# A graph network layer pair: one-hots of the first stage on VectorE in three wide instructions per tile, those of the second in two per two pairs, and a ring reported by quarters

## The reference

```python
def layer0(h, src, dst):                      # GIN
    agg = segment_sum(h[src], dst)            # rows gathered by src, summed by dst
    z = (1.0 + eps_gin) * h + agg
    z = relu(z @ W1 + b1) @ W2 + b2
    z = (z - z.mean(0)) * rsqrt(z.var(0) + 1e-5) * gamma + beta
    return z + h

def layer1(x, row, col, val):                 # here row = src, col = dst
    support = segment_sum(val[:, None] * x[col], row)
    return relu(support @ weight)

x = layernorm(x + layer0(x, src, dst))
x = layernorm(x + layer1(x, src, dst, edge_weight))
```

## Time and profile before

| | |
|---|---|
| timed runs | 4326.99, 4327.98, 4332.28 us; median 4327.98 us |
| span of the profiled execution | 5351.1 us, 79415 instructions; no time other than its span is given for it |
| busy in the profile | PE 3721.5, POOL 3177.6, DVE 2301.2, ACT 1495.5 us |
| granted PE clock, mean | 0.83 of 2.4 GHz |
| gathers | 1664 in stage 1, 1612 in stage 2 |
| moved by DMA | 541 MB, 101 GB/s on the mean |

### The profile page before, as it was taken

The page is one execution under the profiler, slowest core; times in us unless marked ns, Lnnn a source line. Parts: engine busy times, 40 slices in busy tenths (PEclk is TensorE's granted clock), DMA queues, the critical chain, the costliest instruction groups (busy, mean ns, idle before and its releaser), DMA issues.

```text
span 5351.1 us, 79415 instructions
## 1 busy us (share of the span) xinstructions
PE 3721.5 (70%) x16131; PEld 3045.6 (57%) x16132; DVE 2301.2 (43%) x5448; ACT 1495.5 (28%) x4377; POOL 3177.6 (59%) x3352
## 2 busy tenths in 40 slices
PE   2677676667667776767742667777777777777777
PEld 2565555555555655656632556566665666665666
DVE  2545454545555544545563233333333333333333
ACT  2444444445444444444552000000000000000001
POOL 6666655565656665666335666666666666666662
PEclk6887888888887878888855789888888888888898
DMA  4333333333333333333293333333333333333331
GB/s 134 93 97 92 99 90 97 90 97 93 95 93 97 93 97 91 96 97 99 62 298 123 90 94 99 96 101 96 100 101 99 95 100 100 102 97 97 100 100 53
DMA packets 298112, 541.14 MB, mean 101 GB/s; under 512 B 77802, under 2 KB 190302, under 8 KB 297838
## 3 DMA queue, kind: packets, MB, share of 16 engines
q0 software_dynamic: 159424, 434.52, 28.3%
q10 hardware_dynamic: 89348, 67.77, 4.0%
q1 hardware_dynamic: 49066, 36.39, 2.2%
HBM read 489.80 MB, written 46.88 MB: 100 GB/s over the span
## 4 chain that ended last, share of the span: by engine, by line
issue 27%; ACTq 16%; another core or an unknown queue 15%; PE 15%; ACT 12%; DVE 9%; DVEq 4%; DMA 2%; SPq 1%; POOL 0%; PEldq 0%; POOLq 0%
PE ps L1419 10%; ACT ones_sb L1613 7%; DVE work L1096 7%; ACTq L1611 4%; ACTq L1613 2%; DVEq L1096 2%; PE ps L1221 2%; ACT ring L1611 2%; ACTq L1642 1%; PE ps L1459 1%; ACT ones_sb L1619 1%; ACTq L1617 1%; ACTq L377 1%; PE ps L1292 1%
## 5 line engine op out<-in xcount | busy, mean ns | idle before, releaser
L548 POOL DMA_INDIRECT ring<-in_x,idx x1664 | 1587.9, 954 | 1039.5 <-issue 456.4
L606 POOL DMA_INDIRECT ring<-x_dram,idx x1612 | 1528.0, 948 | 904.9 <-issue 479.8
L1419 PE MATMUL ps<-ring,work 128*128 x6448 | 1631.3, 411 | 581.1 <-DVE work L1096 387.5
L1419 PEld LDWEIGHTS ps<-ring,work 128*128 128x128 f32 x6448 | 1327.7, 208 | 851.0 <-issue 649.4
L1221 PE MATMUL ps<-ring,ones_sb 128*128 x3708 | 1115.7, 449 | 454.8 <-ACT ones_sb L1619 301.9
L1096 DVE TENSOR_SCALAR work<-ps,dstT,wT 128x256 f32<-128x256 f32 x1612 | 748.0, 536 | 1551.6 <-remote 977.0
L1221 PEld LDWEIGHTS ps<-ring,ones_sb 128*128 128x128 f32 x3708 | 800.4, 225 | 676.6 <-issue 550.2
L1613 ACT ACTIVATE ones_sb<-tile_nodes,dstT 128x128 f32<-128x128 f32 x1854 | 651.0, 391 | 396.5 <-issue 331.1
L1292 PE MATMUL ps<-work 128*128 128x128 f32 x3384 | 499.2, 301 | 203.6 <-issue 148.1
L1292 PEld LDWEIGHTS ps<-work 128*128 128x128 f32 x3384 | 484.0, 216 | 233.5 <-issue 189.8
L1791 ACT ACTIVATE work<-ps 128x512 f32<-128x512 f32 x49 | 29.3, 597 | 1764.2 <-remote 1111.7
(11 more groups left out here) (240 smaller groups left out, 2299.3 us busy)
## 6 DMA issues: line engine op xcount, KB each, us to landing
ring<-in_x,idx POOLq DMA_INDIRECT x1664
ring<-x_dram,idx POOLq DMA_INDIRECT x1612
z_dram<-z_pair ACTq DMA_DIRECT2D x49, 256.0 KB
ones_sb<-x_dram ACTq DMA_DIRECT2D x49, 256.0 KB
ring<-z_dram SPq DMA_DIRECT2D x24, 512.0 KB, 4.1
ring<-in_x SPq DMA_DIRECT2D x24, 512.0 KB, 5.6
x_dram<-ring ACTq DMA_DIRECT2D x24, 512.0 KB
out<-ones_sb ACTq DMA_DIRECT2D x48, 256.0 KB
```

Source lines behind the costliest of these rows:

```text
L548: nc.gpsimd.indirect_dma_start(out=ring[:, q, c, :], out_offset=None, in_=x, in_offset=bass.IndirectOffsetOnAxis(ap=idx[:, q, c:c + 1], ax ...
L606: nc.gpsimd.indirect_dma_start(out=ring[:, q, c, :], out_offset=None, in_=x1_dram, in_offset=bass.IndirectOffsetOnAxis(ap=idx[:, q, c:c + ...
L1419: last = nc.tensor.matmul(to[:, t * D:(t + 1) * D], ones_of[:, b, c, t * P:(t + 1) * P], ring[:, ds((p + b) & (RING - 1), 1), c, :].rearra ...
```

## The change

- Stage 1's one-hots move from ACT to DVE (`ones_of_tile` in the vector block). A one-hot is now `(dstT + tile_base) == minus_iota`, one instruction for many chunks, with the destinations and the node numbers broadcast: one instruction for the shared pair (256 elements per partition), one for all eight head pairs (2048), one for the last (256), and 512 elements per two loop pairs. The tile's `tile_base` is the scalar. They are made whether the tile has such pairs or not; the table's counts become fixed numbers per tile (`TILE_ONES` = 10).
- DVE makes the first half of `keyed(k - 1)`, then the one-hots of tile 2k+1, the second half, and after `take(k)` those of tile 2k+2. It waits for the sum of the tile two before.
- The self weights are copied by POOL, eight pairs at a time, from `self_next`, which SP loads beside `idx`.
- Stage 2: for two pairs one instruction `equal` over 1024 elements (bucket_nodes in PSUM, dstT in SBUF) and one product with wT in place, with a wait between; a wait for the heads of the bucket before stands ahead of the first four loop pairs.
- Four semaphores per ring instead of sixteen: SP reports eight pairs at a time. POOL waits for slots every four pairs.
- PE waits once for a tile's head one-hots and twice for its landed pairs (`low`, `end`). ACT's order becomes simpler.
- `table` and `table2` are 16-bit.

```diff
+        tile_base = sb("tile_base", [P, NT], f32)
+        minus_iota = sb("minus_iota", [P, P], f32)
+        self_next = sb("self_next", [P, RING, 2], f32)
...
-                        for g in range(RING // TWO):
-                            sp.wait_ge(s_gathered[g], r * (32 * TWO) + 32 * TWO)
-                            sp.sem_inc(s_landed, TWO)
...
+                        for g in range(4):
+                            sp.wait_ge(s_gathered[g], r * (32 * QUARTER) + 32 * QUARTER)
+                            stand(sp)
+                            sp.wait_ge(s_selfed, r * 4 + g + 1)
+                            sp.sem_inc(s_landed, QUARTER)
+                            if g % 2 == 1:
...
+                                sp.dma_start(self_next[:, h * HALF:(h + 1) * HALF, :],
+                                             selfT[:, ds((i + 1) * RING + h * HALF, HALF), :]).then_inc(s_idx[h], 16)
...
+            def selves_of(q, of):
+                nc.gpsimd.tensor_copy(ring_self[:, q:q + QUARTER, :], of[:, q:q + QUARTER, :]).then_inc(s_selfed, 1)
...
-                        if q % TWO == 0:
-                            pool.wait_ge(s_entered, r * RING + (q - RING + 3))
+                        if q % FOUR == 0:
+                            pool.wait_ge(s_entered, r * RING + (q - RING + FOUR + 1))
...
+                        if (q + 1) % QUARTER == 0:
+                            selves_of(q + 1 - QUARTER, self_next)
...
+            def ones_of_tile(j, bank):
+                new, head, m4, m2, _, _, _, shared, off, sweep = entry(dve, j)
...
+                def equal(to, at, n):
+                    return nc.vector.scalar_tensor_tensor(
+                        out=to.rearrange("p b c n -> p (b c) n"),
+                        in0=dstT[:, ds(at, n), :].rearrange("p b c -> p (b c)").unsqueeze(2).to_broadcast([P, 2 * n, P]),
+                        scalar=base, in1=minus_iota[:, :].unsqueeze(1).to_broadcast([P, 2 * n, P]), op0=ALU.add, op1=ALU.is_equal)
+                if not (isinstance(j, int) and j < 2):
+                    dve.wait_ge(s_acc, j - 1)
+                equal(shared_of[bank], shared, 1).then_inc(s_onehot, 1)
...
+                equal(heads_of[bank], head, BATCH)
+                equal(last_of[bank], m2, 1).then_inc(s_onehot, TILE_ONES - 1)
...
                 def weighted(to, p, n):
-                    for b in range(n):
-                        for c in range(2):
-                            last = nc.vector.tensor_scalar(to[:, b, c, :], bucket_nodes, dstT[:, ds(at + b, 1), c], wT[:, ds(at + b, 1), c],
-                                                           ALU.is_equal, ALU.mult)
-                    last.then_inc(s_onehot2, n)
+                    wide = [P, 2 * n, BUCKET]
+                    each = lambda of: of[:, ds(at, n), :].rearrange("p b c -> p (b c)").unsqueeze(2).to_broadcast(wide)
+                    nc.vector.tensor_tensor(flat_of, bucket_nodes.unsqueeze(1).to_broadcast(wide), each(dstT), ALU.is_equal).then_inc(s_equal2, n)
+                    dve.wait_ge(s_equal2, p + n)
+                    nc.vector.tensor_tensor(flat_of, flat_of, each(wT), ALU.mult).then_inc(s_onehot2, n)
...
+                pe.wait_ge(s_onehot, head + counted + TILE_ONES)
+                pe.wait_ge(s_landed, low + first)
```

More of the change, by code:

```diff
@@ L15 @@
 TWO = 2
+QUARTER = RING // 4
+FOUR = 4
 GROUP = 4
@@ L859, in take, with keyed @@
                 stand(dve)
-            def keyed(k):
-                for q in range(PARTS):
+            def keyed(k, parts):
+                for q in parts:
                     mine = slice(q * WIDTH, (q + 1) * WIDTH)
@@ L973, in block @@
                 if old >= 1:
-                    keyed(k - 1)
+                    keyed(k - 1, range(PARTS // 2))
+                ones_of_tile(2 * k + 1, 1)
+                if old >= 1:
+                    keyed(k - 1, range(PARTS // 2, PARTS))
                 if old >= 5:
@@ L987, in _ @@
                 block(k, 5, False)
-            keyed(NS - 1)
+            keyed(NS - 1, range(PARTS // 2))
+            ones_of_tile(2 * NS + 1, 1)
+            keyed(NS - 1, range(PARTS // 2, PARTS))
+            ones_of_tile(2 * NS + 2, 0)
+            ones_of_tile(2 * NS + 3, 1)
             regions_and_targets()
@@ L1206, in sum_tile @@
             def sum_tile(j, bank, others):
-                new, head, m4, m2, end, off, _, rep, _, _ = entry(pe, j)
+                new, head, m4, m2, end, low, rep, _, off, sweep = entry(pe, j)
+                first = sweep * RING
+                counted = first + off
                 if not (isinstance(j, int) and j < 2):
```

287 lines of the change are left out of this document (128 added, 159 removed).

## The result

The changed kernel takes **4579.17 us** (median of 4 runs, 4572.48 to 4589.37) against 4327.48 us before (4 runs): ratio **1.058** [1.057, 1.060], 252 us slower. The forecast was 358 us slower. The profiled execution's span is 4575.0 us, so this time the profile is a picture of the timed runs.

A forecast was written before the change was run, and what follows sets the result against it. POOL's gather issue (4108 us) was taken as the bound of the timed 4328 us; 342 for held gathers + 46 copies + 20 late reports - 50 spared waits = 358 us more, say 4685 us, range 4330 to 4830.

The forecast's parts named there:

- The 2048- and 256-element one-hots of stage 1: VectorE in stage 1: instructions with both inputs in SBUF hold POOL's gathers, 150 us plus 7 us on the mean.
- The product of stage 2: VectorE in stage 2: products with wT, both inputs in SBUF, hold POOL's gathers, 182 us plus 3 us for single pairs.
- The copies: POOL: 104 self-weight copies between gathers, each 0.14 us plus one gap of 0.30 us, 46 us; ends 15 and 130.
- The late quarters: Ring reports of eight pairs: PE sees the last six pairs of each stage later, 20 us (0 to 20).
- Recovered waits: POOL's waits for PE: a PE fed sooner spares some of 0 to 213 us, taken as 50 us less.
- What VectorE does more: VectorE's added work, to 1708 us in stage 1 and some 1060 in stage 2, is covered by POOL's gathers.
- The equal of stage 2: VectorE in stage 2: bucket_nodes in PSUM against dstT, so it holds no gather and is harmless.
- The wait between equal and product: VectorE in stage 2: 415 waits of at most 1.26 us, 523 us as upper end, still covered.
- (a): Rival: ScalarE's one-hots bound the timed runs, not gather issue; the change would be faster, 4243 us, chance 0.15.
- (b): Rival: gathers don't wait for the new two-SBUF instructions; 4344 us, chance 0.08.
- (c): Rival: gathers wait, but half of it hides in POOL's other waits; 4495 us, chance 0.13.
- (d): Rival: VectorE becomes the bound of stage 1 through dependent steps with waits, 98 us more, 4783 us, chance 0.10.

The follow-up runs named there:

- b2: Kernel before with only the ring changed: reports of eight pairs, slot waits every four pairs, both stages, 16-bit tables; 4358.97 us against 4338.23, ratio 1.0047.
- e2: Changed kernel with stage 1's one-hots reading the node numbers from PSUM instead of SBUF, same instructions and sizes; 4474.24 us, ratio 1.033 to before.
- e1: Changed kernel with stage 2's one-hots made as before, one instruction per chunk with bucket_nodes in PSUM; 4500.76 us, ratio 1.0395 to before.
- e5: Changed kernel with a 512-element PSUM-to-PSUM copy between stage 2's equal and product; 4737.03 us, ratio 1.0914 to before.
- b1: Kernel before with one operand of keyed's long compare (L870) moved from PSUM to SBUF, and 16-bit tables; 4404.99 us against 4330.5, ratio 1.0174.
- e3: Changed kernel with stage 2's old one-hots and stage 1's node numbers read from PSUM, both edits together; 4395.53 us, ratio 1.0146 to before.
- e6: Changed kernel with each self-weight copy cut into two halves without a wait, in the slow batch (before 5431.63 us); 5415.76 us, ratio 0.998.
- e9: Changed kernel with stage 1's 2048-element heads instruction cut into four of 512; 4519.7 us, ratio 1.0444 to before.
- e4: Changed kernel with each of POOL's 104 self-weight copies made twice, with a wait between; 4727.07 us, ratio 1.0896 to before.

## Why the prediction was right, and where it was not

The mechanism was the forecast one: POOL's gather issue is the bound, and gathers wait for VectorE's instructions with two operands in SBUF. Its sizes were not all right.

**The sum, term by term** (forecast, then measured):

- The 2048- and 256-element one-hots of stage 1: 157, measured 138 less the 12 of the kernel before (b2's gathers: 956 against 949 ns) = **126 us**. The phase average is near; e2 takes it away (the 128 us by which stage 1's last gather starts earlier).
- The product of stage 2: 185, measured **78 us** (e1 takes off 78). This is the term that was mis-sized. "Nothing ties one phase to the other for long, so I take the mean" is the step that failed: a held gather sets the phase anew, and at 2.48 us a couple the 245 products that follow another couple directly hold nothing; e5 makes the same products hold 231.
- The copies: 46, measured at most **19 us**: POOL's stage 1 has 25.4 us of copies (3 of them held ones) and 6.8 less idle time than b2's (504.3, 511.1), and of that 19 some 4 are more waiting for PE (13.4, 9.1). The step that took a copy for 0.14 us and a whole issue gap counted a gap that isn't there: the copy lies largely in the one that is.
- The late quarters: 20, measured **21 us** (b2), 13 of it the end and 5 the four further gathers; the size was right in part by luck, since the further gathers weren't in it.
- Recovered waits: -50, measured **0**: b1 and b2 wait for PE's slots for 9 us in stage 1, and the changed kernel for 13. "I take those as the recording's" was wrong in its reason, since a whole batch runs so, though right in what it drew from it: the timed runs were POOL-bound.
- Not in the sum: **6 us** more between the stages (190 against b2's 2288.4 - 2104.0 less a gather = 183).

126 + 78 + 19 + 21 + 6 = 250 of the 252 us; each term is good to a few us (b2 ran in another batch), so that the rest is only 2 is chance. The forecast's nearness is partly luck, too: the 50 us that weren't there to recover hid half of the 107 by which the product's term was too large; without them it would have been 408.

**The other parts.** What VectorE does more (about 350 us in stage 1, 240 in stage 2) cost nothing by itself, as forecast, nor did ScalarE's lost work bring anything. The equal of stage 2 was without effect, as forecast. The mean gather of stage 1 was forecast at 1.04 us and came out at 1.029; that of stage 2 at 1.06, and came out at 0.994. The wait between equal and product cost nothing on POOL. Two readings of the prediction were not exact: 6.26 us over five gathers are 1.252 us, not 1.254 (1.254 is the median of that trace, and 1.251 in the kernel after, which makes 4098 us for 4108); and 16 gathers, not 11, start under L778 in the trace of before, of which the 11 with over 0.13 us of it left were held.

**The rivals.** (a), ScalarE's one-hots as the bound, is out: e3 has VectorE's one-hots with hardly any holding (956 and 945 ns) and is still no faster than before. (b), gathers that don't wait, is out by e1, e2 and b1. The Trainium skill, "SBUF — State Buffer", section "Who interferes with whom", infers that tensor_tensor with two SBUF inputs doesn't stall descriptor generation, since it takes only the read interface; here it delays gathers, by 78 us (L1160), by 74 in b1 (L870), and a broadcast operand holds as well as a plain one. The prediction called the inference "against L885"; that goes further than the trace. A gather reads its 128 indices from SBUF, so the section's other sentence that the prediction gives, on a GpSimd instruction that reads SBUF, may cover it. Whether the reading of the indices is what is held, or something else in the gather, no run here can tell. (c), half hidden, gives 4495 (4515 with the 20 us of the quarters, which its sum leaves out); the time lies between it and the forecast, but nothing was hidden in these runs: it was less contention, not cover. In the batch of 5432 us, the variant e6 had all of it covered. (d), VectorE as the bound of stage 1, may be present in small: about 25 us that e2, e3 and e9 give back at the end of stage 1, behind the held gathers, if the reading of e2 is right.

## What to carry to other kernels

When a chain of indirect gathers is the bound, count the VectorE instructions with both operands in SBUF, not VectorE's busy time: move one operand to PSUM, or cut long instructions, since a gather is held only until the end of the one that runs. Moving a broadcast constant into PSUM took 105 us off here and added no instruction; the opposite move, of another instruction's operand, made the kernel before 1.7% slower. Where such instructions recur at a fixed distance, don't average over their phase: start from a held gather and work out where the next ones fall. And if the profiled span isn't near the timed median, ask first for a profile that is.

## What the runs showed of the hardware that was not expected

- The phase of two engines' loops isn't free: a held gather starts the next one 1.12 us behind the product's end, and the couple's length then decides. The same 391 products of 1.23 us held 78 us at 2.48 us a couple and 231 at 3.09, where the mean over phases gives 182; the 245 that follow a couple directly held 0 and 143.
- A short copy between two gathers on POOL costs 0.07 us in the median (1.32 against 1.25), two half-sized ones 0.18 (1.43); a wait for the last copy adds 0.8 us of idle time ahead of the next two gathers (e4). A copy on POOL is held by VectorE's two-SBUF instructions like a gather (up to 2.23 us instead of 0.22).
- One batch of runs had TensorE idle ahead of single matmuls in straight-line code, about 1 us each (L1371), and a kernel 25% slower (5432 against 4329 us), with gathers (949 ns median), copies and VectorE's instructions (947 against 950 ns for `keyed`'s compare) as long as ever. In it the kernels' order was another one: the heads in four came out slower than the halved copies (5516 and 5416 us), elsewhere faster (4520 and 4594).
